# Stores on another queue, later x loads, split residual loads and an earlier lora reload in a fused attention and QLoRA kernel

## The reference

```python
q = X @ Wq.T + bq;  k = X @ Wk.T + bk;  v = X @ Wv.T + bv
scores = where(j > i, -inf, q @ k.T / sqrt(1024))
x = layernorm(X + softmax(scores, axis=-2) @ v)
h = x
for blk in range(3):               # qlora(x, i) = x @ W[i].T + b[i] + (x @ la[i].T) @ lb[i].T
    y = gelu(layernorm(qlora(h, 2 * blk)) * g[blk] + b[blk])
    h = qlora(y, 2 * blk + 1) + h
out = layernorm(x + h)             # W[i] = (q[i] / 7.5 - 1) * repeat(scale[i], 16)
```

## Time and profile before

| | |
|---|---|
| Median of 3 runs | 1378.18 us (1376.76 to 1498.4) |
| The profiled execution, its own time | 1375.92 us |
| Span of the profiled core (core 2, the slowest) | 1374.4 us |
| Spans of cores 0 to 7 | 1373.4, 1365.1, 1374.4, 1371.2, 1370.8, 1370.2, 1365.4, 1370.5 us |
| Granted clock of cores 0 to 7 | 0.982, 0.986, 0.981, 0.979, 0.985, 0.981, 0.987, 0.981 |
| PE busy | 1297.8 us (94%) |
| DVE, ACT, POOL busy | 698.6 (51%), 712.3 (52%), 393.9 us (29%) |
| POOL's scaling, lines 425 and 427 | 48 x 1061 ns and 48 x 2354 ns |
| DMA: SP's queue, POOL's queue | 141.84 MB in 51808 packets, 53.62 MB in 19456 |

### The profile page before, as it was taken

The page is one execution under the profiler, slowest core; times in us unless marked ns, Lnnn a source line. Parts: engine busy times, 40 slices in busy tenths (PEclk is TensorE's granted clock), DMA queues, the critical chain, the costliest instruction groups (busy, mean ns, idle before and its releaser), DMA issues.

```text
span 1374.4 us, 21020 instructions; the slowest of 8 cores (1365.1 to 1374.4 us)
## 1 busy us (share of the span) xinstructions
PE 1297.8 (94%) x6611; PEld 608.3 (44%) x6740; DVE 698.6 (51%) x1459; ACT 712.3 (52%) x1075; POOL 393.9 (29%) x308
## 2 busy tenths in 40 slices
PE   5999999898999999999999999998899999999997
PEld 2444444343444444444444444445444444444454
DVE  3136556443344566436562473478535624744785
ACT  2234115562202165535864884676678648846753
POOL 0133444664953355433000057000100000570000
PEclk9899999999999999999999999999999999999999
DMA  8985646797955445594101057016621010560023
GB/s 249 170 225 185 216 130 173 187 247 235 327 181 194 137 154 188 195 317 166 62 0 62 1 159 208 2 62 215 239 99 62 1 62 0 161 184 24 1 93 154
DMA packets 71371, 196.80 MB, mean 143 GB/s; under 512 B 6032, under 2 KB 14816, under 8 KB 68192
## 3 DMA queue, kind: packets, MB, share of 16 engines
q1 hardware_dynamic: 51808, 141.84, 32.6%
q0 software_dynamic: 19456, 53.62, 13.2%
HBM read 158.85 MB, written 46.15 MB: 149 GB/s over the span
## 4 chain that ended last, share of the span: by engine, by line
PE 79%; DMA 5%; DVE 5%; issue 4%; ACT 4%; POOL 2%; SPq 1%; DVEq 0%; ACTq 0%; POOLq 0%
PE ps L217 79%; ACT POOLT L221 3%; DMA x1s<-POOLT 2%; DVE POOLT L225 2%; DMA POOLT<-wq 1%; DVE SM L1062 1%; SPq L105 1%; DMA POOLT<-xt 1%; POOL POOLT L701 1%; DMA POOLT<-lb_h 1%; DVE SM L234 1%; DMA POOLT<-qw_t 1%; POOL POOLT L427 0%; DVEq L111 0%; ACT L221 0%
## 5 line engine op out<-in xcount | busy, mean ns | idle before, releaser
L217 PE MATMUL ps<-POOLT 128*128 128x512 bf16 (+3 forms) x5476 | 1226.9, 376 | 35.5 <-ACT POOLT L221 11.0
L217 PEld LDWEIGHTS ps<-POOLT 128*128 128x128 bf16 x5600 | 533.9, 99 | 663.1 <-issue 90.5
L221 ACT ACTIVATE POOLT<-ps,SM 128x512 bf16<-128x512 f32 (+4 forms) x396 | 262.8, 683 | 311.4 <-PE ps L217 188.2
L225 DVE TENSOR_TENSOR POOLT<-POOLT 128x512 bf16<-128x512 bf16 (+1 forms) x448 | 249.1, 592 | 210.1 <-ACT POOLT L221 185.4
L225 DVE TENSOR_TENSOR POOLT<-ps,POOLT 128x512 bf16<-128x512 f32 (+1 forms) x186 | 123.6, 688 | 156.1 <-PE ps L217 104.2
L1020 POOL TENSOR_TENSOR POOLT<-POOLT 128x512 f32<-128x512 f32 x64 | 88.9, 1419 | 372.4 <-ACT POOLT L221 193.2
L221 ACT ACTIVATE POOLT<-POOLT 128x512 bf16<-128x512 f32 (+3 forms) x186 | 125.8, 687 | 125.1 <-DVE POOLT L225 73.0
L221 ACT ACTIVATE POOLT<-POOLT,SM 128x512 bf16<-128x512 f32 (+2 forms) x120 | 109.7, 918 | 135.2 <-DVE SM L228 90.7
L221 ACT ACTIVATE POOLT<-POOLT,CF 128x512 bf16<-128x512 bf16 x192 | 154.2, 807 | 26.6 <-DVE POOLT L225 25.9
L234 DVE SCALAR_TENSOR_TENSOR POOLT<-ps,SM,POOLT 128x512 f32<-128x512 f32 x128 | 96.2, 751 | 87.0 <-PE ps L217 86.7
L217 PE MATMUL ps<-POOLT,CB 128*128 128x512 bf16 (+2 forms) x331 | 96.0, 384 | 29.5 <-DVE POOLT L225 18.9
(11 more groups left out here) (56 smaller groups left out, 288.2 us busy)
## 6 DMA issues: line engine op xcount, KB each, us to landing
POOLT<-qw_t SPq DMA_DIRECT2D x48, 512.0 KB, 5.3
POOLT<-sc_t SPq DMA_DIRECT2D x48, 512.0 KB, 6.4
POOLT<-weffs SPq DMA_DIRECT2D x24, 1024.0 KB, 8.7
POOLT<-xt SPq DMA_DIRECT2D x16, 1024.0 KB, 8.9
x1s<-POOLT POOLq DMA_DIRECT2D x16, 1024.0 KB, 9.0
POOLT<-x1s SPq DMA_DIRECT2D x8, 2048.0 KB, 11.9
POOLT<-x1s SPq DMA_DIRECT2D x64, 256.0 KB, 3.2
out<-POOLT POOLq DMA_DIRECT2D x28, 512.0 KB, 3.1
```

The source lines that it names most:

```text
L217: return pe.put(lambda e: e.matmul(out, lhsT, rhs, start=start, stop=stop), *after, sig=sig)
L221: return act.put(lambda e: e.activation(out, in_, func, bias=bias, scale=scale, accum_out=acc), *after)
L225: return dve.put(lambda e: e.tensor_tensor(out, a, b, op), *after)
```

## The change

Four edits. Stores of effective weight tiles are issued from ScalarE's queue instead of GpSimd's. Tiles 1 to 3 of the second sequence's x are asked for inside `pv_chunk`, tiles 1 and 2 after the pieces and x1 stores of the chunk before have been put on the queue, tile 3 after output tile 3 of chunk 3; tile 0 stays after row 3. `load_r` takes one half at a time; for chunks 2 and 3 the second half is asked for after output tile 5 instead of 2. `load_lora` is called at the end of `dq_lora` instead of in `dq_finish`.

```diff
@@ dq_lora
             dq_tok[k] = toks
+            if k in (15, 31):
+                load_lora(2 * (k // 16) + 2)
@@ dq_finish
             dq_free[s] = (t,)
-            if k in (15, 31):
-                load_lora(2 * (k // 16) + 2)
-            do_free[s] = pool.dma(s_do[s], weffs[w, c], do, t)
+            do_free[s] = act.dma(s_do[s], weffs[w, c], do, t)
@@ load_r
-        def load_r(seq, ic):
-            for h, g in enumerate(x_groups(4 * seq + ic)):
-                k_rl[(seq, ic, h)] = sp.dma(
-                    s_rl[g], RG[g].rearrange("p (c t) -> p c t", t=TT),
-                    xsrc[seq][:, 4 * h:4 * h + 4, ic * TT:(ic + 1) * TT], rg_free[g])
+        def load_r(seq, ic, h):
+            g = x_groups(4 * seq + ic)[h]
+            k_rl[(seq, ic, h)] = sp.dma(
+                s_rl[g], RG[g].rearrange("p (c t) -> p c t", t=TT),
+                xsrc[seq][:, 4 * h:4 * h + 4, ic * TT:(ic + 1) * TT], rg_free[g])
+
+        k_x_next = [None] * 4
@@ pv_chunk, after the work of output tile et
                 if (ic, et) in ((1, 2), (2, 2)):
                     while pieces:
                         pieces.pop(0)()
-                    load_r(seq, ic + 1)
+                    load_r(seq, ic + 1, 0)
+                    if seq == 0:
+                        k_x_next[ic] = load_x(1, ic, ic, xt_read[ic])
+                if (ic, et) in ((1, 5), (2, 5)):
+                    load_r(seq, ic + 1, 1)
+                if (seq, ic, et) == (0, 3, 3):
+                    k_x_next[3] = load_x(1, 3, 3, xt_read[3])
@@ main loop (the other calls of load_r issue both halves in a row, as before)
-                    if seq == 0 and jt % 4 == 3:
-                        k_x_next[jt // 4] = load_x(1, jt // 4, jt // 4, xt_read[jt // 4])
+                    if seq == 0 and jt == 3:
+                        k_x_next[0] = load_x(1, 0, 0, xt_read[0])
```

More of the change, by code:

```diff
@@ L852, in build_program @@
                 k_bvc = centre_bv(k_bv)
-                load_r(0, 0)
-                load_r(0, 1)
+                for h in range(2):
+                    load_r(0, 0, h)
+                for h in range(2):
+                    load_r(0, 1, h)
                 for ic in range(4):
@@ L867, in build_program @@
                     if ic == 0:
-                        load_r(1, 0)
+                        for h in range(2):
+                            load_r(1, 0, h)
                     if ic == 2:
@@ L871, in build_program @@
                             pieces.pop(0)()
-                        load_r(1, 1)
+                        for h in range(2):
+                            load_r(1, 1, h)
                 c_bias(seq, sl)
                 v_chunk(seq, 3, sl[3])
-            k_x_next = [None] * 4
             prev = None
```

## The result

| | before | after |
|---|---|---|
| median time, us (20 runs each) | 1378.19 | 1381.07 |
| lowest | 1374.92 | 1378.72 |
| span of the profiled execution, us | 1374.4 (core 2) | 1378.4 (core 5) |
| spans of its eight cores, mean, us | 1370.1 | 1373.0 |
| PE busy on core 5, us | 1307.0 | 1308.3 |

The ratio after/before is 1.0026, with an interval of 1.0017 to 1.0034. I had forecast 9 us less.

What follows compares the result with a forecast made beforehand. PE was taken as the bound, with 76.6 us idle. Core 3, slowest after returning 9.5, gives 1361.7; plus 2 for ACT and 2 for returning waits 1365.7; with measurement offsets 1369 us, range 1360 to 1381.

Steps and rivals of the forecast that it cites:

- Stall A: PE's 8.54 us wait until 277.87 on core 2, behind a late weight store; its removal to return 9.9 us.
- The qw_t load behind it leaves on time: On SP's queue behind the second residual half: shorter blocking lets the weight load leave on time, ending POOL's 18 us wait.
- My own last sign of being wrong: DVE waiting for POOL's scaling by 5 us and more between 255 and 310: loads, not stores, set the pace.
- POOL does not stand 18 us, and D goes: With qw_t on time, POOL's 18.14 us wait until 328.97 ends; 4.2 us returned on core 2.
- D: PE's 2.64 us stall until 342.03 on core 2, through late POOL scaling; 4.2 us to return with the half clock.
- B: PE's 2.02 us stall until 319.56 on core 2, DVE waiting for chunk 3's first residual half; all to return.
- Cost 0, the cover is over 50 us: Sequence 2's x tiles, issued later, still land over 50 us before they are read, so moving them costs nothing.
- Rival 3: ACT becomes the bound in softmax rows and chunk ends, slower than before: 1389, or 1407 with all stores exposed; chance 0.10.
- Plus 2 of waits that come back: From 250 to 300 the DMA engines are near full, with about 10 us less for the same bytes: 2 us lost.
- The lora factors: Earlier reload cannot issue sooner, so the 1.57 us stall at 409.58 stays; net 0, at best 1.6 and the clock dip.
- Rival 2: SP still blocks on the second half's x1 store, qw_t is late and D remains: about 1372; chance 0.12.
- Rival 1: DMA engines are the limit, stall A stays in part, giving 1 to 2 instead of 6: 1374; chance 0.17.

Runs made afterwards that it cites:

- w2_x_chunk3_pool: w1_x_chunk3 with the effective weight stores back on POOL's queue; mean core span 1362.0 us, 6.4 below the kernel before.
- w1_x_chunk3: Changed kernel with x tiles 1 to 3 spread over chunk 3 and sequence 2's residual loads later; mean core span 1357.3 us, ratio to before 0.9938.
- h7_half_late: Changed kernel with the second residual half asked for after output tile 7 instead of 5, both chunks; mean core span 1359.9 us, 8.5 below before.
- v1_wload_act: Changed kernel with the qw_t and sc_t loads issued by ScalarE instead of SP; mean core span 1367.1 us, -0.9 +- 3.7 to before, three runs.
- v2_no_x: Changed kernel with the loads of sequence 2's x tiles 1 to 3 left out; mean core span 1356.7 us, 11.3 below before.
- y1_x3_early: Changed kernel with x tile 3 issued together with tile 2 in chunk 2; mean core span 1368.0 us, 0.4 below before.
- v3_r_late: Changed kernel with the residual loads of sequence 2's chunks 0 and 1 asked for later; mean core span 1364.9 us, 3.1 below before.

## Why the prediction was wrong, by its own steps

- **Stall A: right.** I said 6.4 us for core 3 and 9.9 for core 2; by PE load 1400 they had gained 6.0 and 7.7, the mean of the eight cores 7.8, and the window of core 5 went to 19.28 busy at clock 1.00. The store lands as I took it, in 7.5 us in the median. The Trainium skill's rule that I weighed against it (DMA: Bandwidth & Descriptors, section Issuing engines are not separate DMA queues), by which only issue time is saved, doesn't hold here: `w2_x_chunk3_pool` against `w1_x_chunk3` is 4.7 us from the issuing engine alone. The other half of that section, that all share the same 16 DMA engines and interleave, agrees with the traces: without the x tile on POOL's queue SP's weight load lands in 8.9 to 11.6 us instead of 16.3 to 19.1. With the Trainium skill's section Queues, rings and completion order on the same page, round robin between queue rows, the stores agree: landings of at most 12.4 us against 20.9 (core 2).
- **"The qw_t load behind it leaves on time": this step failed, and with it the sign.** It does leave in time, at 268.12. I stopped at the issue and didn't follow the load to its landing. Two residual halves are in front of it in the same queue, in a stretch where the DMA engines are full and an x tile is under way beside them, and it needs 19.1 us. I had the row that warned of it: 22.7 us for an x load on POOL. I used it for POOL's queue only. Price: 7.3 us, where the sum had nothing but a share of the 2 us of waits that come back. `h7_half_late`, `v1_wload_act` and `v2_no_x` show it.
- **My own last sign of being wrong came true.** I had named DVE waiting for POOL's scaling by 5 us and more between 255 and 310; it waited 6.38 us, until 291.82 on core 5. The loads set the pace, as that sentence says.
- **"POOL does not stand 18 us, and D goes"; "together 6.2 us" for B and D.** B is gone: 2.8 us in the mean of the cores, against 2.02 for core 2. SP's row shrank to 7.6 us, and the weight load behind it leaves at 309.62 instead of about 320 (core 5 against core 2). But it lands 15.5 us later, behind the same two halves, and POOL still stands 16.05 us. D went on cores 0 and 2, 4.4 and 4.3 us against the 4.2 that I said for core 2, and not on core 3, for which I had counted 2.6. The mean of the cores gained 0.5 between 321 and 353.
- **"Cost 0, the cover is over 50 us" for x: failed.** True for the tile's readers. The question that I didn't ask was what stands behind the tile in POOL's queue: chunk 2's x1 stores, for which SP's next residual waits, and behind that the next weight load. I had tile 3 issued near 319, 20 us ahead of those stores; it was issued at 335.92, the first store at 339.84. Price: 6.5 us, shown by `y1_x3_early` and `v3_r_late` from both ends. Tile 1, in the crowd near 262, is besides one of the two things that the stall at 290 needs. I had put the two megabyte-long neighbours, tile and store, down as no longer in each other's way, which held for chunks 0 and 1 and not for chunk 2.
- **ScalarE's issues.** I took 0.45 us each, it is 0.36, and no experiment can tell the 2 us that I charged from 0. Rival 3, slower through ACT, has the right sign and the wrong mechanism.
- **"Plus 2 of waits that come back".** This was the term for what really decided. It measured 7.3 + 6.5 = 13.8 us. I had no row behind the 2; the bound was to be had: the weight load behind SP's 18.04 us row was as late as stall A was long, so all of A could be given back.
- **The lora factors.** As said, the `lb_h` stall stays (1.57 before, 1.4 after). Whether the place in front of the scaling costs something is not settled: POOL stands 9.86 us for PE at its first reload (row below, after again, core 5), yet the edit alone was not slower.

```profile
232.16 0.59 POOL L105 DMA_DIRECT2D POOLT<-la_h  x1 [9.86 <-PE ps L217]
```

- **PE's idle time.** The 76.6 us that I set as the bound are too many: the busy time of core 2 lacks 129 matmul records. On core 5, where none are missing, it is 1370.2 - 1307.0 = 63.2 us. No term of the sum rests on it.
- **Rivals 1 and 2.** Rival 2 (SP still blocks) named the right victim, `qw_t`, and half of the mechanism; it priced it as a gain not made, not as a new stall. Rival 1 (the DMA engines as the limit) is wrong where it says that A stays, and right in that the crowd near 270 has a price: the stall at 290 goes when the x tile is taken out of that stretch. It is not a limit over the whole: `w1_x_chunk3` moves the same bytes, at other times, and no PE wait of over 1 us is left between 255 and 385 on the cores compared.

## What to carry to other kernels

A stall that is removed moves everything behind it closer to its due time: before counting it as gain, find the next load that was late anyway and was covered by it, and bound the gain by its slack. For each DMA that is moved, follow what stands behind it in its queue to its landing, not to its issue, and whoever waits on that semaphore on to the next queue. Put loads that have a due time in front of bulk loads that have none for a long while, and keep such bulk off the other queues in a stretch where the engines are full. Here swaps of the first kind were worth 10.9 us against the changed kernel (8.5 against the one before), and the whole order about 14 (11).

## What the hardware showed that I had not expected

- Within one queue a 512 KB load took 19.1 us behind 2 MB (core 5, 17.5 on core 2); with one of these megabytes behind it instead, it took 11.7 us and its reader on POOL began 6.8 us sooner (core 2). With both in front and a 1 MB load on another queue gone, it took 10.3 (core 2 of `w1_x_chunk3`).
- At a DMA share of 1.05, PE lost 0.1 us in 20 when the order was right (`w1_x_chunk3`, 320 to 340), and at 1.03 a store on POOL behind a load needed 23.4 us (after, from 340).
- A DMA issue on ScalarE's queue took 0.36 us, about SP's 0.33 and well under POOL's 0.59.
